# Last cross-attention of a Flamingo-like block: half of the scores go through ScalarE head by head, and the null key's product gets 128 rows

## What is computed

```
q = heads(x_normed @ Wq) * scale          # 16 heads of 64, from 128 features
k, v = heads(split(context @ Wkv))        # context (8, 32, 256) after the reshape: 64 keys per batch element
k = concat(null_k, k); v = concat(null_v, v)          # one learned null key in front
attn = softmax(q k^T)                     # over 65 keys, per head
out = heads_joined(attn v) @ Wout
out = layernorm(out) * ln_scale + ln_bias
x = x + tanh(g_xattn[3]) * out
```

## Time and profile before

| | |
|---|---|
| median of the runs | 1058.12 us (3 runs, 1058.01 to 1060.27) |
| profiled execution | 1058.48 us |
| span of its instructions | 1056.8 us |
| busy in the span | PE 815.1 us (77%), DVE 655.7 us (62%), ACT 372.7 us (35%), POOL 359.1 us (34%) |
| mean granted clock of PE | 0.866 of full |
| the loop over the 16 tiles | 863.7 us (first scores) to 958.6 us (last null product), 94.9 us |

### The profile page before, as it was taken

The page is one execution under the profiler, slowest core; times in us unless marked ns, Lnnn a source line. Parts: engine busy times, 40 slices in busy tenths (PEclk is TensorE's granted clock), DMA queues, the critical chain, the costliest instruction groups (busy, mean ns, idle before and its releaser), DMA issues.

```text
span 1056.8 us, 14563 instructions
## 1 busy us (share of the span) xinstructions
PE 815.1 (77%) x5027; PEld 551.5 (52%) x5027; DVE 655.7 (62%) x1850; ACT 372.7 (35%) x746; POOL 359.1 (34%) x490
## 2 busy tenths in 40 slices
PE   2727999356877788887989499788798998994374
PEld 1716888223444444443359466568343665773363
DVE  4683222347677777754977668996467338996321
ACT  2123444035555565661441534342200234441210
POOL 5324442565454442203854101102000004544254
PEclk9857999758989999998999599895899888996597
DMA  8506775100000000000000000000000050002220
GB/s 207 221 0 197 203 220 166 38 12 11 11 9 11 1 1 2 1 2 1 0 1 2 0 1 1 1 1 1 1 0 0 1 160 0 1 1 80 65 60 28
DMA packets 51770, 45.44 MB, mean 43 GB/s; under 512 B 6804, under 2 KB 47655, under 8 KB 51442
## 3 DMA queue, kind: packets, MB, share of 16 engines
q1 hardware_dynamic: 48146, 36.91, 11.9%
q0 software_dynamic: 3552, 7.61, 2.7%
HBM read 36.90 MB, written 7.80 MB: 42 GB/s over the span
## 4 chain that ended last, share of the span: by engine, by line
PE 56%; DVE 23%; issue 8%; POOL 6%; ACT 4%; DMA 3%; POOLq 0%; SPq 0%; DVEq 0%; ACTq 0%
PE psum L2388 6%; PE psum L1095 4%; PE psum L2013 3%; PE psum L1386 3%; PE psum L2603 3%; PE psum L2633 2%; DVE stats L149 2%; DVE XN L163 2%; PE psum L583 2%; PE psum L1363 2%; PE psum L1300 2%; PE psum L255 2%; DVE scratch L1627 2%; PE psum L1106 2%; DVE XN L1928 2%
## 5 line engine op out<-in xcount | busy, mean ns | idle before, releaser
L1627 DVE TENSOR_REDUCE scratch<-psum 128x2 f32<-128x512 f32 (+1 forms) x160 | 107.6, 686 | 62.5 <-PE psum L1343 40.9
L1545 ACT ACTIVATE scratch<-psum 128x512 f32<-128x512 f32 x160 | 94.0, 602 | 94.9 <-PE psum L1363 93.4
L219 POOL TENSOR_SCALAR veps<-moments 128x4 f32<-128x4 f32 x44 | 8.6, 195 | 306.9 <-DVE moments L152 303.0
L255 PE MATMUL psum<-ident,XN 128*128 128x128 f32 x144 | 31.3, 361 | 57.3 <-DVE XN L163 48.8
L876 DVE SCALAR_TENSOR_TENSOR scratch<-psum,b_block_bias,scratch 128x256 f32<-128x256 f32 (+1 forms) x48 | 18.6, 429 | 74.1 <-ACT scratch L1020 69.7
L943 POOL DMA_INDIRECT scratch<-pair_rows,b_gather_at x39 | 39.2, 1004 | 71.2 <-PE psum L1068 44.4
L2388 PE MATMUL psum<-late,scratch 128*128 128x512 f32 x128 | 58.4, 619 | 5.7 <-DVE routing_wide L2331 5.0
L2537 POOL TENSOR_TENSOR scratch<-scratch,arena 128x1024 f32<-128x1024 f32 x16 | 30.4, 1901 | 92.0 <-DVE arena L2757 92.0
L1343 PE MATMUL psum<-arena 128*128 128x512 bf16 x128 | 52.0, 414 | 5.1 <-ACT arena L1525 3.0
L1363 PE MATMUL psum<-scratch,arena 128*128 128x256 bf16 x256 | 50.6, 281 | 6.4 <-ACT scratch L1531 4.4
L255 PEld LDWEIGHTS psum<-ident,XN 128*128 128x128 f32 x144 | 22.0, 188 | 64.0 <-issue 31.1
(11 more groups left out here) (441 smaller groups left out, 2052.6 us busy)
## 6 DMA issues: line engine op xcount, KB each, us to landing
arena<-in_L_ffn_w SPq DMA_DIRECT2D x72, 128.0 KB
arena<-in_L_ffn_wg SPq DMA_DIRECT2D x24, 256.0 KB
wide<-in_L_xattn_Wkv SPq DMA_DIRECT2D x1, 2048.0 KB
wide<-in_L_ffn_W SPq DMA_DIRECT2D x1, 2048.0 KB, 8.7
late<-in_L_ffn_W SPq DMA_DIRECT2D x8, 256.0 KB, 6.3
pair_results<-scratch SPq DMA_DIRECT2D x15, 128.0 KB
X<-in_x SPq DMA_DIRECT2D x2, 512.0 KB, 5.0
C<-in_ctx SPq DMA_DIRECT2D x2, 512.0 KB, 6.6
```

Source lines behind the costliest of these rows:

```text
L255: last = t.transpose(c.bank[self.banks[g % 2]][:, i * P:(i + 1) * P], self.src[:, GROUP * g + i, :], c.ident[:])
L1545: a.activation(out, bank[3 + e % 2][:, :], ACT.Exp).then_inc(s["exp"], 1)
L1627: v.tensor_reduce(out, bank[m % 3][:, :].rearrange("p (h t) -> p h t", t=n), AX.X, ALU.max, negate=True).then_inc(s["maxed"], 1)
```

## The change

Three things change in `NullStage`.

1. The null key's product gets 128 rows: `null_vals` and `null_probT` are no longer cut to 16 partitions. The rows past the 16th are set to zero once, in `prepare`, by two more POOL instructions.
2. Heads 0 to 7, in the first PSUM bank of a tile, are no longer shifted by DVE. DVE computes the negated maximum (`negate=True`, then a minimum with the negated null scores), and ACT takes each of these heads from PSUM with the negated maximum as the bias of the exponential: eight instructions of 128 x 64. DVE adds the negated maximum to heads 8 to 15 alone, and ACT's ninth instruction takes these and the 16 null values, 528 in all, in place.
3. Since ACT now reads a score bank too, `scores(j)` waits for `exp` of tile j - 2 as well as for `shifted`.

```diff
@@ NullStage.__init__
-        self.null_vals = ar.take(D)[0:16, :]
-        self.null_probT = ar.take(2 * P)[0:16, :].rearrange("p (u n) -> p u n", u=2)
+        self.null_vals = ar.take(D)
+        self.null_probT = ar.take(2 * P).rearrange("p (u n) -> p u n", u=2)
@@ prepare (POOL)
         self.zero_others(g, self.kv)
+        padded = c.pool_chain
+        padded.link(g, g.memset(self.null_vals, 0.0))
+        padded.link(g, g.memset(self.null_probT.rearrange("p u n -> p (u n)"), 0.0))
@@ pe, scores(j)
             if j >= 2:
                 t.wait_ge(s["shifted"], 2 * (j - 1))
+                t.wait_ge(s["exp"], j - 1)
@@ act
-        a.activation(self.null_vals, bank[1][0:16, 0:D], ACT.Copy).then_inc(s["nulls_copied"], 1)
+        a.activation(self.null_vals[0:16, :], bank[1][0:16, 0:D], ACT.Copy).then_inc(s["nulls_copied"], 1)
...
         def exponentials(j):
+            u, first, late = j % 3, bank[2 * (j % 2)], slice(512, 1040)
             a.wait_ge(s["shifted"], 2 * j + 2)
-            a.activation(self.prob[:, j % 3, :], self.prob[:, j % 3, :], ACT.Exp).then_inc(s["exp"], 1)
+            for h in range(8):
+                keys = slice(64 * h, 64 * h + 64)
+                a.activation(self.prob[:, u, keys], first[:, keys], ACT.Exp, bias=self.top[:, u, h:h + 1])
+            a.activation(self.prob[:, u, late], self.prob[:, u, late], ACT.Exp).then_inc(s["exp"], 1)
...
-            a.activation(self.null_probT[:, j % 2, :], bank[4 + j % 2][0:16, P:2 * P], ACT.Copy) \
+            a.activation(self.null_probT[0:16, j % 2, :], bank[4 + j % 2][0:16, P:2 * P], ACT.Copy) \
                 .then_inc(s["p_turned"], 1)
@@ dve, softmax(j)
-            own.link(v, v.tensor_reduce(top, main_in, AX.X, ALU.max))
-            own.link(v, v.tensor_tensor(top, null_in, top, ALU.max))
+            own.link(v, v.tensor_reduce(top, main_in, AX.X, ALU.max, negate=True))
+            own.link(v, v.tensor_tensor(top, null_in, top, ALU.min))
             if j >= 3:
                 v.wait_ge(s["p_t"], 3 * (j - 2))
-            v.tensor_tensor(main, main_in, bc(top[:, :, None], (P, 16, 64)), ALU.subtract) \
+            v.tensor_tensor(late, late_in, bc(top[:, 8:16, None], (P, 8, 64)), ALU.add) \
                 .then_inc(s["shifted"], 1)
-            v.tensor_tensor(null, null_in, top, ALU.subtract).then_inc(s["shifted"], 1)
+            v.tensor_tensor(null, top, null_in, ALU.subtract).then_inc(s["shifted"], 1)
...
-        own.link(v, v.tensor_copy(self.null_scores, bank[5][:, 0:256]))
+        own.link(v, v.tensor_scalar(self.null_scores, bank[5][:, 0:256], -1.0, None, ALU.mult))
```

More of the change, by code:

```diff
@@ L2734, in softmax @@
             null_in = self.null_scores[:, 16 * j:16 * j + 16]
-            main = self.prob[:, u, 0:1024].rearrange("p (h n) -> p h n", n=64)
+            late_in = bank[2 * (j % 2) + 1][:, :].rearrange("p (h n) -> p h n", n=64)
+            late = self.prob[:, u, 512:1024].rearrange("p (h n) -> p h n", n=64)
             null = self.prob[:, u, 1024:1040]
```

## The result

| | before | changed |
|---|---|---|
| median of the runs | 1058.12 us (5 runs, 1057.71 to 1060.27) | 1052.37 us (5 runs, 1050.63 to 1053.40) |
| ratio, with its 95% interval | | 0.9938 [0.9922, 0.9954] |
| profiled execution, span | 1058.48, 1056.8 us | 1053.10, 1051.4 us |
| loop, from the first scores to ACT's last result | 863.71 to 958.64: 94.93 us | 865.50 to 953.83: 88.33 us |
| first scores to the transposes of tile 2 | 25.85 us | 23.23 us |

5.75 us faster by the medians, 0.6%. The start of the loop gives 2.62 us, the eleven tiles of the middle 3.03 and the end 0.95, together 6.60; what comes ahead of the loop took 1.8 us more in this execution, and what comes behind 0.6 less. The stretch ahead varied from 861.4 to 865.8 us over all profiles of this study, in which no kernel changes much there.

The account below looks back on a forecast made before the run. The prediction took PE to bound the loop at 5.05 us a tile. Gains of 0.3 at the start, 3.5 from null products, and 0.4, 0.27 and 0.2 at the end sum to 4.7 us: 1058.12 to 1053.4 us, range 1050.2 to 1056.4.

Parts of the forecast that it names:

- PE bounds the loop: In the middle tiles PE's matmuls fill all 5.05 us, so work taken from DVE gains nothing there by itself.
- The null product, 0.27 us a tile: On PE, three steps around the null matmuls shrink from 0.61 to 0.34 us with 128 rows.
- a gain of nothing: Lower bound for the null product if row count does not matter; as a rival 9%, 1057.5 us.
- The slack of the round through DVE and POOL stays about 0.5 us: Between POOL's division and PE's transposes: PE's side loses 0.55 us, the round loses 0.53, so slack stays.
- the null product does not pay alone: In the middle tiles, two shorter null products, 0.55 us, would eat the 0.57 slack without DVE's halved subtraction.
- ACT's nine instructions are hidden: On ACT, eight at 0.256 us and one at 0.60, together 2.65, end 0.42 us before the result is wanted.
- Start 0.3 us, clock neither way: At tiles 0 and 1, earlier first transposes gain 0.3 us by tile 1; no clock gain or loss is counted.
- the sum of 4.7: Whole loop: 0.3 at the start, 3.5 from 13 null products, then 0.4, 0.27 and 0.2 us at the end.
- the better clock: At tile 1, full clock again for `scores(3)` would be worth up to 1.7 us; not counted.
- The two null products at the start, 0.5 us: On PE ahead of tile 2's transposes, two of the 13 null products counted at 0.27 us each.
- The end, 0.9 us: Last tiles: 0.4 us from tile 13 to 14, 0.27 in tile 14, 0.2 in tile 15.
- Added waits and memsets at nothing: Only `scores(2)` is held, at little cost; POOL's memsets, about 0.2 and 0.32 us, hide in a 38.56 us wait.

Follow-up runs that it names:

- exp_only: The full change with the null product cut back to 16 rows; median 1055.41 us, ratio to before 0.9975.
- adds_first: The full change with POOL's four additions of the layer norm's shift done ahead of its 16 divisions; median 1050.99 us, ratio to before 0.9932.
- old_start: The full change, but tiles 0 and 1 keep the old full subtraction, single exponential and waits; median 1053.36 us, ratio to before 0.9956.
- all16: The full change with all 16 heads through ACT and DVE subtracting only the null values; median 1052.36 us, ratio to before 0.9943.
- adds_first_early: The full change with POOL's additions ahead of its divisions and ACT's eight narrow exponentials waiting for the maximum alone; median 1048.75 us, ratio to before 0.9909.

## Why the prediction came out right

The forecast was 1053.4 us, the measured median is 1052.37, within the range of 1050.2 to 1056.4. By its steps:

- *PE bounds the loop.* Right; exp_only takes work from DVE and leaves the tile at 5.05 us.
- *The null product, 0.27 us a tile.* The mechanism is right, the size a little low: 0.34, with what the transposes behind it gained (1.09 to 1.04 us). Of the two pages of the Trainium skill that I weighed, TensorEngine Tiling (Array Packing), Key Properties, says that a change of tiling mode drains the engine, and the runs agree with it in that what costs is going from 128 rows to fewer and back, and 16, 32 and 64 cost the same. The drain itself stands in no row; what the rows show is the load that no longer begins ahead of its matmul. TensorE: Matmul & The Clock Gate (Step-by-step: what each phase is for) says that the row count does not matter for a load's time, and that holds too (183 and 192 ns). My step from there to a gain of nothing did not follow.
- *The slack of the round through DVE and POOL stays about 0.5 us.* Right where nothing disturbs it: POOL ends at 931.42 and PE starts the transposes at 931.84. At the first tiles of the middle it was mis-sized. I took DVE's short instructions at 0.17 us, and they are held up while POOL divides or adds. In the changed kernel seven of the eleven tiles from 2 to 13 take 4.76 to 5.04 us instead of 4.71. In sum the middle gained 3.03 us against 11 x 0.27 = 2.97 forecast: the null product gave 11 x 0.07 = 0.8 us more, and these delays took 0.7 back. adds_first brings every tile to 4.71, so it is through POOL's additions that the delays reach PE. That the null product does not pay alone was right, and stronger than I had it: alone it gains nothing in the middle. The halved subtraction takes 1.22 - 0.69 = 0.53 us out of the ring of 4.97 us, which leaves an estimate of 4.44, below the tile of 4.71.
- *ACT's nine instructions are hidden.* Right: 0.196 us a piece against 0.256, 2.2 us in all against 2.65, 0.95 us of margin against 0.42.
- *Start 0.3 us, clock neither way.* This is the term that failed. With two null products at 0.27 the sum had 0.84 us up to tile 2, and 2.62 were measured; these 1.78 us are most of the 1.9 by which the loop (6.60) beat the sum of 4.7. All 2.62 come with the eight heads on ACT and the halved subtraction, for exp_only has them too; 2.01 of them go again with old_start. By PE's timelines the first transposes start 0.78 us sooner after the first scores (I had 0.4 to 0.5), the stretch from there to the first value matmuls is 2.50 us shorter, nearly all of it clock, and 0.66 is lost again before tile 2, where PE waits for POOL. I had named the better clock as worth up to 1.7 us and counted none of it; the earlier trace rows give (1.97 - 1.09) + (3.44 - 1.88) = 2.44 for it. I had also put the maximum of tile 2 within 0.3 us of its old place, and it came 1.16 later.
- *The two null products at the start, 0.5 us.* With the old start they save 0.61 (25.24 against 25.85), with the new one nothing, since PE then waits for POOL: the change and exp_only both take 23.23 us to tile 2.
- *The end, 0.9 us*: 0.95 measured. *Added waits and memsets at nothing*: only `scores(2)` waits, for 2.56 us; the table of waits shows no other one of PE on the exponentials.

The middle and the end were forecast to within 0.1 us each, though in the middle two errors of 0.8 and 0.7 us cancelled. That the median came within 1.0 us of the forecast is partly luck: the start alone was off by 1.78 us, and the medians then gained 0.85 us less than the loop of the profiled execution.

## What to carry to other kernels

Where PE bounds a loop, look at the steps from start to start of its matmuls, not at their durations: one product with fewer rows between full ones stood out there by 0.1 us a step. Before you shorten the bound engine, work out the next round, and with it what the instructions on it will overlap after the shift; two changes that are worth 0.5 and 3 us of loop alone were worth 6.6 together. Where DVE has a short instruction with all operands in SBUF in front of a long one, see what POOL is doing at that moment.

## What the runs showed of the hardware

- An f32 product with 16, 32 or 64 rows between products with 128 rows costs PE 0.34 us more at full clock than the same product filled up with zero rows to 128 (tiles of 5.05 against 4.71 us), whatever the number of rows. The load of its first matmul, and that of the first matmul behind it, do not begin 0.11 us ahead of the matmul as they do with 128 rows.
- DVE's 128 x 16 operation with both inputs and its output in SBUF takes 0.17 us alone. Beside a POOL operation it took up to 0.90 us (a division of 1.90 us) and 1.18 us (an addition of 1.28 us, in all16), and ended when that ended (887.93 against 887.90, 912.32 against 912.29). One of 1,024 columns whose main input is PSUM, with a small one from SBUF, kept its 1.23 us beside the same division. The Trainium skill, in SBUF — State Buffer (SBUF: two separate sides), says that VectorE and GpSimd share a pair of ports that is an exclusive lock, and that a VectorE operation with two SBUF inputs contends for it with a GpSimd operation that reads SBUF; the trace agrees in both cases.
- An exponential of 128 x 64 from PSUM with a bias operand lasts 288 ns, and they follow each other at 196 ns.
- The granted clock behind a gap in PE's work came out differently with the place of the work before it. With `scores(2)` 0.68 us behind `scores(1)` and then 4.58 us of waiting the transposes ran at half clock (granted 0.50 in old_start). With 2.56 us of waiting before `scores(2)` and 0.49 behind it they ran at full clock (1.00), at the price of `scores(2)` itself (3.42 us against 1.98). With 1.75 and 2.48 us both ran at full clock (adds_first_early). What decides between these was not tested.
